# A cross network over 128 tiles of rows: four of the 4 MB loads issued as nine transfers of every ninth partition

## The reference

```
x0 = inputs                      # 16384 x 4096
def step(x, wb):
    wi, bi = wb                  # 4096 x 1, 4096
    xw = matmul(x, wi)           # one number per row
    x_new = x0 * xw + bi + x
    return x_new
x = scan(step, inputs, (w, b))   # 6 layers
```

## Time and profile before

| what | value |
|---|---|
| median of three timed runs | 1295.48 us |
| the profiled execution's own time | 1288.29 us |
| its span, first to last instruction | 1286.3 us |
| VectorE busy | 1165.9 us, 91% |
| TensorE matmul busy | 783.3 us, 61% |
| bytes moved by DMA | 537.37 MB, 418 GB/s over the span |
| time of their packets, as a share of 16 engines' span | 50.2% loads, 48.6% stores |
| TensorE's granted clock | 0.774 of full speed |

### The profile page before, as it was taken

How to read it: one execution, slowest core, us unless ns; L and a number is a source line. 1 busy time by engine, 2 the same in 40 slices (tenths; PEclk the granted TensorE clock), 3 DMA queues, 4 the chain that set the end, 5 groups by cost and what they waited for, 6 DMA issues and landing times.

```text
span 1286.3 us, 20063 instructions
## 1 busy us (share of the span) xinstructions
PE 783.3 (61%) x9114; PEld 732.1 (57%) x9114; DVE 1165.9 (91%) x652; ACT 100.1 (8%) x340; POOL 4.3 (0%) x17
## 2 busy tenths in 40 slices
PE   7667666655575566566665655655665575555743
PEld 4667666655565465565565555555655475555643
DVE  5999999999898898998988989889989898898986
ACT  2000000000000000000000000000000000000010
POOL 1000000000000000000000000000000000000000
PEclk9777777787768877777777778778687868777677
DMA  9999999999999999999999999999999999999996
GB/s 383 411 370 420 432 437 429 436 430 433 431 433 436 431 433 426 436 426 432 421 425 419 409 417 420 417 431 420 428 426 411 417 431 421 411 401 424 428 420 249
DMA packets 19890, 537.37 MB, mean 418 GB/s; under 512 B 2241, under 2 KB 2241, under 8 KB 2849
## 3 DMA queue, kind: packets, MB, share of 16 engines
q1 hardware_dynamic: 9648, 268.44, 50.2%
q10 hardware_dynamic: 10224, 268.74, 48.6%
HBM read 268.73 MB, written 268.44 MB: 418 GB/s over the span
## 4 chain that ended last, share of the span: by engine, by line
DMA 64%; DVE 26%; PE 7%; issue 1%; ACT 1%; ACTq 0%; DVEq 0%; SPq 0%
DMA out_dram<-tiles 36%; DMA tiles<-in_r_inputs_dram 27%; DVE blocks L268 14%; DVE tiles L291 11%; PE dots L411 5%; PE turned L380 1%; ACT spread L202 1%; DMA tiles<-in_L_rec_b_dram 1%; PE dots L369 1%; PE strips L359 0%; DVE scale L279 0%; ACTq L185 0%; DVEq L46 0%; ACT growth L212 0%; ACTq L183 0%
## 5 line engine op out<-in xcount | busy, mean ns | idle before, releaser
L411 PE MATMUL dots<-blocks,weights 128*64 128x128 f32 x7808 | 666.5, 350 | 378.0 <-DVE blocks L268 377.9
L411 PEld LDWEIGHTS dots<-blocks,weights 128*64 128x64 f32 x7808 | 633.4, 186 | 401.8 <-DVE blocks L268 401.4
L268 DVE STREAM_TRANSPOSE blocks<-tiles 128x2048 f32<-128x2048 f32 x256 | 576.1, 2289 | 100.7 <-DMA tiles<-in_r_inputs_dram 97.0
L291 DVE SCALAR_TENSOR_TENSOR tiles<-tiles,scale,scratch 128x2048 f32<-128x2048 f32 x129 | 299.9, 2326 | 0.0
L291 DVE SCALAR_TENSOR_TENSOR tiles<-tiles,scale,c_low 128x2048 f32<-128x2048 f32 x129 | 298.7, 2316 | 0.2
L202 ACT ACTIVATE spread<-dots,group_mask 128x128 f32<-128x128 f32 (+1 forms) x268 | 75.4, 364 | 1074.3 <-PE dots L411 989.5
L380 PE MATMUL turned<-layer_sel,spread 128*128 128x8 f32 x512 | 68.1, 259 | 86.1 <-ACT spread L202 86.1
L380 PEld LDWEIGHTS turned<-layer_sel,spread 128*128 128x128 f32 x512 | 62.4, 191 | 102.0 <-issue 96.2
L369 PE MATMUL dots<-blocks,weights 128*64 128x64 f32 x768 | 32.8, 267 | 20.1 <-DVE blocks L268 20.1
L369 PEld LDWEIGHTS dots<-blocks,weights 128*64 128x64 f32 x768 | 32.1, 181 | 22.0 <-issue 22.0
L212 ACT ACTIVATE growth<-turned,ones 128x16 f32<-128x16 f32 (+1 forms) x67 | 18.3, 273 | 78.8 <-PE turned L380 78.8
(11 more groups left out here) (24 smaller groups left out, 11.5 us busy)
## 6 DMA issues: line engine op xcount, KB each, us to landing
tiles<-in_r_inputs_dram SPq DMA_DIRECT2D x61, 4096.0 KB, 24.7
out_dram<-tiles ACTq DMA_DIRECT2D x61, 4096.0 KB, 35.3
tiles<-in_r_inputs_dram SPq DMA_DIRECT2D x6, 2048.0 KB, 26.9
out_dram<-tiles ACTq DMA_DIRECT2D x5, 2048.0 KB, 12.8
out_dram<-tiles ACTq DMA_DIRECT2D x4, 512.0 KB, 5.9
tiles<-in_L_rec_w_dram ACTq DMA_DIRECT2D x1, 96.0 KB
tiles<-in_L_rec_b_dram ACTq DMA_DIRECT2D x4, 24.0 KB
tiles<-in_L_rec_b_dram ACTq DMA_DIRECT2D x1, 96.0 KB
```

Of the source, the lines that this page charges most:

```text
L268: nc.vector.transpose(blocks[:, p % PLACES, :], source).then_inc(blocks_ready, 1)
L291: done = nc.vector.scalar_tensor_tensor(out=tile[:, at], in0=tile[:, at], scalar=scale[:, u % 2, t, L - 1:L], in1=c, op0=ALU.mult, op1=ALU ...
L411: last = nc.tensor.matmul(dots[at:at + KM * Q, :, :, :], weights[:, c * CH // Q + k:c * CH // Q + k + KM, :], place[:, :, k * Q:(k + KM) * Q],
```

## The change

`spared(q)` is true for pairs 7, 25, 43 and 61. Their load is no longer one transfer of 128 partitions but nine: number `r` takes partitions `r`, `r + 9`, `r + 18` and so on. The first two have 15 partitions each, the other seven 14; together they are the same 128 partitions and the same 4 MB. VectorE's wait for a landing now counts nine transfers for such a pair (`landings`). SyncE's wait for stores still uses `transfers`, as no store is changed.

```diff
--- before.py
+++ after.py
@@ -19,6 +19,8 @@
 N_SLOTS = 5
 HEAD, TAIL = 2, 4
 STORE_PARTS = 4
+STEP = 9
+EVERY, FIRST = 18, 7
 
 
 def cross_network(nc, x, w, b, out):
@@ -128,8 +130,14 @@
         def pieces_before(u):
             return 2 * tiles_of(u)[0]
 
+        def spared(q):
+            return q % EVERY == FIRST and not in_singles(q)
+
         def transfers(q, t):
             return sum(1 for k in range(q % N_SLOTS, q + 1, N_SLOTS) if t == 0 or in_singles(k))
+
+        def landings(q, t):
+            return sum(STEP if spared(k) else 1 for k in range(q % N_SLOTS, q + 1, N_SLOTS) if t == 0 or in_singles(k))
 
         def weights_of(g):
             rows = slice(g * Q, (g + 1) * Q)
@@ -151,6 +159,9 @@
                 if in_singles(q):
                     for t in range(TB):
                         sp.dma_start(tiles[:, s, t, :], x_pairs[q, :, t, :]).then_inc(x_landed[s][t], 16)
+                elif spared(q):
+                    for r in range(STEP):
+                        sp.dma_start(tiles[r:P:STEP, s, :, :], x_pairs[q, r:P:STEP, :, :]).then_inc(x_landed[s][0], 16)
                 else:
                     sp.dma_start(tiles[:, s, :, :], x_pairs[q]).then_inc(x_landed[s][0], 16)
 
@@ -270,7 +281,7 @@
             def wait_tiles(u):
                 first = tiles_of(u)[0]
                 q, t = first // TB, first % TB
-                dve.wait_ge(x_landed[q % N_SLOTS][t], 16 * transfers(q, t))
+                dve.wait_ge(x_landed[q % N_SLOTS][t], 16 * landings(q, t))
 
             def scan(u):
                 n_of = tiles_of(u)[1]
```

## The result

The change made the kernel slower by 1.1%, where 0.4% had been forecast:

| | before | after |
|---|---|---|
| median of four timed runs | 1295.01 us | 1308.81 us |
| lowest to highest | 1293.4 to 1298.59 | 1306.98 to 1313.46 |
| ratio, with its 95% interval | 1 | 1.0108 [1.0072, 1.0144] |
| profiled execution, its span | 1288.29, 1286.3 us | 1307.11, 1305.3 us |

A forecast was written before the change was run, and what follows sets the result against it. The prediction took one slow DMA engine's own packet list as the bound. Four added rows at 1.25 us gave 5.0 us, other terms 0: 1295.48 + 5.0 = 1300.5 us, 0.4% more, range 1271 to 1308 us.

The forecast's parts named there:

- One slow engine bounds the kernel: Whole run: one DMA engine some 3% slower than the rest; cost 18 us from 600 to 1200 us, 8.9 us at end.
- The slow engine is among the six, and not spared: Slow engine carried the 6-row bias transfers; with nested sets it gets nine rows per changed load instead of eight.
- The rival of a spared slow engine: Changed loads leave the slow engine 32 rows fewer in all; 1273 us at the median, chance 0.25.
- Who gets how many rows: Each changed load: 14 engines get nine rows instead of eight, one two, one none; 2689 small packets, 10096 on loads' queue.
- Four rows, 5.0 us: Slow engine gets one added row per changed load, four in all at 1.25 us, each paid in full.
- Engines do not starve: Between the nine issues of a changed load, engines alternate with stores, a row every 2.4 us; cost taken as 0.
- 0.33 to 2.12: SyncE's issue times in us for the small loads, 0.33 median to 2.12 at most; nine are 3 to 19 us, hidden.
- 29 us of loss as the other end: Rival at the changed loads: slow issues starve the engines, 7.3 us per load, 1330 us in all; chance 0.08.
- a row in a small transfer lasts 1.21 us: Changed loads: 32 KB row time taken from 432 GB/s, 27.0 GB/s per engine; 1.25 us on the slow engine.
- 600 to 1200 us stays near 419: Sign that the slow engine keeps its rows: GB/s at share 1.00, with VectorE waits over 4 us before the last load.
- about 430, no lone engine near the end: Sign of a spared slow engine: GB/s from 600 to 1200 us, no 0.06-share windows, VectorE's 97 us wait shrinks.
- A share under 1.00 with a dip: Sign of starving engines: DMA share and GB/s fall just after 105, 463, 821 and 1181 us.

## Why the prediction was wrong

**One slow engine bounds the kernel: right in part.** If each packet record of the trace before is joined to the one that starts where it ends, sixteen chains come out, one for each engine. From 200 to 300 us fifteen of them moved 27.08 GB/s and one 26.53. So there is one slow engine, and it is 2.0% slower, not 3%. Sixteen engines at its pace move 424 GB/s, and 419 were measured from 600 to 1200 us. The two queues of before from 600 to 900 us:

```profile
q1 hardware_dynamic: 2159, 62.92, 51.5%
q10 hardware_dynamic: 2163, 63.01, 48.7%
```

A load's row lasted 1.29 us there and a store's 1.22. From 600 to 800 us each of the sixteen chains had loads' rows of 1.27 to 1.31 us at the mean. Why the loads' rows wait longer than the slow engine's own pace asks is open. For the sum it matters little: an added row cost 1.27 us (0.9 to 1.6), where 1.25 was used.

**The slow engine is among the six, and not spared: right, as far as shown.** Added rows on a set of eight cost 19 us; that it is among six is not shown. The rival of a spared slow engine (1273 us) falls with that, and with eight column pieces, which have the same recovery and spare nobody.

**Who gets how many rows: right.** 2688 small packets were counted, 2689 forecast; 10096 packets on the loads' queue, as forecast:

```profile
q1 hardware_dynamic: 10096, 268.44, 49.4%
```

**Four rows, 5.0 us: right in size** (5.1, between 3.6 and 6.5), and only 37% of the loss.

**Engines do not starve: right in effect, on wrong numbers.** Issues took 0.76 to 2.7 us, where 0.33 to 2.12 had been reckoned with, and 29 us of loss as the other end. But what issues cost was not shown to be anything: shorter ones went with a larger loss.

**The failed step: a row in a small transfer lasts 1.21 us.** The working took the time of a row from whole loads and moved it to small ones, and priced everything else at 0. It asked which engines get the rows, and never which partitions they write at that moment. Nor did the range allow for it. No row of the trace before shows a load over part of the partitions beside others of its kind, so the step should have been bounded like an unknown. In its place the runs showed longer rows: 13.8 - 5.1 = 8.7 us of loss, 0.24 us for each of the 36 transfers, where it was 1.90 - 1.22 = 0.68 us with the loads alone. With it the sum is 1295.0 + 5.1 + 8.7 = 1308.8 us; the 8.7 is what is left of the loss. The packets confirm its order in one place: from 484 to 515 us the loads' 164 rows lasted 1.60 us instead of 1.22, which is (1.60 - 1.22) x 164 / 16 = 3.9 us of each engine behind one changed load, where 8.7 / 4 = 2.2 us is the mean.

**The signs would have misled.** "600 to 1200 us stays near 419" was to mark the forecast and "about 430, no lone engine near the end" the spared engine. Of the second sign the rate came (427) without its cause, while VectorE's waits grew from 97.0 to 116.3 us instead of shrinking. A share under 1.00 with a dip was to mark starving; 0.96 came, and the column pieces have 0.94 and lose nothing. A likely account is that a late landing stops VectorE once for 16 to 18 us, the other engines run dry, and the slow engine catches up with its lag; column pieces do the same with equal rows. That is argued, not shown. A sign must not be one that any stall would give.

**Turns were not thought of, and cost nothing.** From 127 to 141 us after, just behind the first changed load, the stores' queue moved 3.47 MB and the loads' 2.13:

```profile
q10 hardware_dynamic: 106, 3.47, 59.7%
q1 hardware_dynamic: 120, 2.13, 40.5%
```

Before, from 110 to 124 us, it was even:

```profile
q10 hardware_dynamic: 96, 3.15, 52.1%
q1 hardware_dynamic: 105, 3.08, 51.0%
```

Each mark takes a turn of its queue: in the joined records of before, from 200 to 300 us, 87 of 88 marks of loads stand between two rows of stores. So a load with more marks lands later. Column pieces land as late, for free.

**Still open.** Why every seventh partition runs at 225 GB/s; whether the small transfers meet at the partitions they write or at the memory they read; why loads' rows took 1.29 us from 600 us on in the kernel before; and whether the same engine is slow in all timed runs.

## What to carry to other kernels

Cut a large load along its columns, not along its partitions: in this kernel eight column pieces of all 128 partitions cost 0.1% or nothing, eight row groups 1.6%. When a load must be moved from an engine, price two things, the rows that the others gain and the pace at which the remaining groups are written, and get the second from a loads-only run of ten lines, which showed it about twice as large as the full kernel did. A dip or a long wait on an engine with idle time to spare is no loss until a control with the same dip is slower.

## What the runs showed of the hardware

- Loads in halves of the partitions run at 209 GB/s against 431 for whole ones, though all 16 engines are at work (share 1.00); in blocks of 14 or 15 partitions at 105.
- The share of busy engines says nothing of this: it is 1.00 at 431, 210 and 209 GB/s, and 1.01 at 225. The bytes must be read beside it.
- One of the 16 engines was 2.0% slower than the others (26.53 against 27.08 GB/s from 200 to 300 us of the kernel before).
- An issue of 14 or 15 rows took 0.76 us at the least where they lay nine apart, and 0.34 us where they were neighbours; one of 128 rows 0.33 us.
- The time from issue to landing moved between the queues. 4 MB stores took 35.3 us before and 26.6 after, whole loads 24.7 us and 31.8. The rows of before, then of after (KB each, median us):

```profile
out_dram<-tiles ACTq DMA_DIRECT2D x61, 4096.0 KB, 35.3
```

```profile
out_dram<-tiles ACTq DMA_DIRECT2D x61, 4096.0 KB, 26.6
tiles<-in_r_inputs_dram SPq DMA_DIRECT2D x57, 4096.0 KB, 31.8
```

A store and a load sum to 60.0 us before and 58.4 after, so here a landing time by itself is no measure of a queue's pace.
